# New step orders for every slot of a 58-slot interleaved kernel

## The chip, the core and the metric

The kernel runs on one core of a Trainium2 chip. A core has a matrix engine (PE in the profile, with PEld for its weight loads), a vector engine (DVE), an activation engine (ACT), a general engine (POOL), and SP, which here only issues DMAs. Each engine works through its own instruction list strictly in order and waits on semaphores. The metric is device time in microseconds (us), the median over executions.

## What is computed

The input x has 4 sequences of 512 tokens by 128 features. Twelve sub-blocks follow each other, each adding to x:

```python
x = x + 0.5 * L0_ffn(ln(x));  x = x + L0_attn(ln(x));  x = x + 0.5 * L0_ffn(ln(x))   # pattern FFN, local attention
x = x + 0.5 * L1_ffn(ln(x));  x = x + L1_attn(ln(x));  x = x + 0.5 * L1_ffn(ln(x))   # top-2 of 8 experts, linear attention
x = x + 0.5 * L2_ffn(ln(x));  x = x + L2_attn(ln(x));  x = x + 0.5 * L2_ffn(ln(x))   # routed experts, block attention
x = x + 0.5 * L3_ffn(ln(x));  x = x + L3_attn(ln(x));  x = x + 0.5 * L3_ffn(ln(x))   # two windowed layers, full attention
```

L3_ffn is two layers, so the kernel counts 14 sub-blocks.

## The kernel before

A *unit* is one sub-block on one sequence: 14 x 4 = 56 units, numbered 0 to 55, four sequences of a sub-block one after the other. A unit has three parts. *pre* normalizes x, projects it, makes bf16 pieces of q and k on DVE (`stack_parts`, L431 to L447) and turns them on PE (`turn_stacks`, L529). *core* is the attention or expert work. *post* projects the result back into x. The work is a software pipeline over *slots*: slot k holds the core of unit k (stream a), the pre of unit k + 1 (stream b) and the post of unit k - 1 (stream c). A few slots have further streams: in slots 0 to 2 DVE and SP prepare tables and fill a DRAM buffer (`make_tables`, `split_rows`, `fill_shear`, L2932 to L3012), and from slot 5 on POOL clears a set of semaphores (`keep`).

Each part is written as generators, one for each engine. A `yield` marks the start of a step, a step being some instructions with their semaphore waits. For each engine a merge puts the steps of the streams into one list, and so fixes the order in which that engine issues them. Within a stream the order is always the program's. Where a slot has a written order for an engine, `in_order` follows it: a string such as `c1a2b1` means one step of stream c, two of a, one of b. Where it has none, `weave` picks the stream whose next nominal time is smallest. Nothing else decides the order of work: the waits are in the steps and go with them.

```python
def merge(name, eng, streams, orders):
    if name in orders:
        in_order(name, eng, streams, orders[name])
    else:
        weave(name, eng, streams)
```

Slots -1 to 2 are each a block of their own that ends in a barrier of all engines. Slots 3 to 56 run in one block, where an engine that has finished its list of a slot goes on to the next; at the end of a slot it waits until POOL's `keep` of that slot has cleared a semaphore set (L3140 is the mark of an engine at a slot's end). Before the change slots 3 to 56 name an order (the entry of slot 56 is empty), and slots -1 to 2 are woven.

Lines that the prediction uses: L310 normalizes x with the result of POOL's L328; L336 turns it on PE and L343 (ACT) takes it; L387 to L401 project q, k, v; L606, L631 are PE work of post; L755, L978 spread a row over the partitions in the pattern FFN's post, L773 to L776 (DVE) and L784, L786 (PE) rank it, L820 and L837 (Gelu) are its pre; L1431 to L1437 (DVE), L1445 (ACT, Exp), L1392, L1406 (PE) are the core of the L0 attention; L1678, L1689, L1694 (PE), L1720 (DVE), L1701 (POOL) the core of the L1 attention.

Of the kernel before, what the change touches and what calls it, by code (L numbers as in the profile page):

```python
# [2383 lines left out]
def l3_layer_post(nc, m, lane, a, b, l):  # L2384
# [89 lines left out]
SLOT_ORDERS = {3: 0, 4: 1, 5: 2, 6: 3, 7: 4, 8: 5, 9: 6, 10: 7, 11: 8, 12: 9, 13: 10, 14: 11, 15: 12, 16: 13, 17: 14,  # L2474
# [3 lines left out]
ORDERS = [  # L2478
    {"tensor": "a5b1a1b1a1b1a1b1c1b1c1b1a1b1a1b2a1c1b1c1a1b2a1c1a3b1a3c1b1c1b1c1b1a1c1b1c1a1c1",
     "vector": "b4a2b5a3b1c2b1a1c1b1a1c1a1b1c4b1c2",  # L2480
     "scalar": "b3a1b2a1c1b3c1b8a1",
     "sync": "a1b5"},
    {"tensor": "b1a1b2c1a1b1a1c1b2a2b1a1b1a3b1c1a1b1c2a1b1c1b1a3b1a1c1b1a2b1c1b1c1b1c1a1c1a6",
     "vector": "b4a7b5a1c1a2b1a1c1a2b1c1a1c1a1b1a1c1a2b1a1c1a1c1a1c1a1c1a2b1c1",
     "scalar": "b3c1b2a1c1b2a1b2a2b1a2b1a3b1a2b4a9",
     "sync": "a4b5"},
    {"tensor": "b1a1b1c1b1c1b1a1b1a1c1b1a2b3a2b1c1a2b1a1b1c1a2b2a2b1a1b1a2b1c1a7",
     "vector": "b4c2a3b5a4b1c1a3b1a2b1c1a3b1a9b1c1",
     "scalar": "b7a1b2a1b1a2b1a2b1a3b1c1a1b1a1b1a2b1a7",
# [795 lines left out]
```

## Time and profile before

| what | value |
| --- | --- |
| median of 3 runs | 3191.61 us (3190.63 to 3198.51) |
| profiled execution | span 3199.9 us; no time is recorded for it besides the span |
| PE busy | 2706.5 us, 85% of the span |
| DVE busy | 2234.0 us, 70% |
| ACT busy | 1703.5 us, 53% |
| POOL busy | 846.5 us, 26% |
| mean granted TensorE clock | 0.896 of full speed |

Busy is the time in which an engine executes; where several waits end together the last one is named. PE is the busiest engine, and its idle time is the span less its busy time.

### The profile page before, as it was taken

Reading aid. Unit: us, or ns where it says so; the run is one execution under the profiler, and the core shown is the slowest. Engines: PE = TensorE matmul, PEld = TensorE weight load, DVE = VectorE, ACT = ScalarE, POOL = GpSimd, SP = SyncE. Lnnn points to the kernel's source line nnn. Section 1 sums busy time; section 2 is a strip of 40 time slices with the busy share of each in tenths; the row PEclk is TensorE's granted clock in tenths of the full one; section 3 lists DMA queues with packets and bytes.
Section 4 is the critical chain, followed back from the end, with each engine's and each line's share of the span. In section 5 each row is a group of like instructions: output and inputs, shape, how many; then the busy total and the mean of one; then the engine's idle time right before and its main releaser. Section 6 shows DMA issues by size and latency. Waiting matters only on the chain.

```text
span 3199.9 us, 64237 instructions
## 1 busy us (share of the span) xinstructions
PE 2706.5 (85%) x24501; PEld 1718.2 (54%) x24561; DVE 2234.0 (70%) x5316; ACT 1703.5 (53%) x4158; POOL 846.5 (26%) x875
## 2 busy tenths in 40 slices
PE   5857688898986789998877888899998988999996
PEld 2545455544443444457755787556563332465664
DVE  4756568778876677765566445798887777788883
ACT  2235443565622266643357434677765666676772
POOL 1010001122111221101232114565541112555550
PEclk8767787899977799998899989999998899999997
DMA  2523310000000000026710466110100000101010
GB/s 105 220 38 66 64 53 1 1 1 1 1 1 1 1 1 1 3 101 225 258 32 2 150 213 205 30 25 17 26 16 2 1 1 1 24 16 26 16 33 11
DMA packets 136844, 159.38 MB, mean 50 GB/s; under 512 B 84949, under 2 KB 111829, under 8 KB 135002
## 3 DMA queue, kind: packets, MB, share of 16 engines
q1 hardware_dynamic: 134010, 150.09, 15.7%
q8 instruction: 196, 3.21, 0.4%
q0 software_dynamic: 2048, 4.20, 0.4%
q10 hardware_dynamic: 480, 0.98, 0.1%
q14 instruction: 110, 0.90, 0.1%
HBM read 106.53 MB, written 30.61 MB: 43 GB/s over the span
## 4 chain that ended last, share of the span: by engine, by line
PE 48%; DVE 23%; ACT 9%; issue 7%; POOL 4%; DMA 3%; SPq 2%; DVEq 0%; POOLq 0%; ACTq 0%
DVE nm L1185 5%; PE ps L1144 3%; PE ps L529 3%; PE ps L1919 3%; PE ps L1121 3%; PE ps L2121 3%; ACT hand L494 3%; PE ps L1085 3%; PE ps L2287 3%; PE ps L387 2%; PE ps L606 2%; PE ps L266 2%; SPq L1368 2%; DVE pre L2207 2%; PE ps L1518 1%
## 5 line engine op out<-in xcount | busy, mean ns | idle before, releaser
L1185 DVE TENSOR_REDUCE nm<-ps 128x2 f32<-128x256 f32 (+2 forms) x704 | 427.6, 643 | 91.3 <-PE ps L1085 49.6
L1234 ACT ACTIVATE core<-ps 128x512 f32<-128x512 f32 x672 | 359.9, 589 | 92.6 <-PE ps L1126 56.7
L328 POOL TENSOR_TENSOR rstd<-ve,weights 128x4 f32<-128x4 f32 x80 | 81.0, 1013 | 869.7 <-DVE ve L305 865.7
L2193 POOL TENSOR_TENSOR pre<-pre,sin 128x512 f32<-128x512 f32 x128 | 238.1, 1879 | 255.4 <-ACT pre L2164 216.1
L1085 PE MATMUL ps<-hand 128*128 128x128 bf16 (+4 forms) x989 | 237.0, 315 | 42.6 <-DVE nm L1185 37.7
L494 ACT COPY hand<-ps 64x512 bf16<-64x512 bf16 x336 | 194.6, 579 | 136.9 <-PE ps L529 88.7
L1121 PE MATMUL ps<-hand 128*128 128x128 bf16 (+4 forms) x999 | 213.9, 303 | 11.2 <-ACT hand L494 6.3
L2327 ACT ACTIVATE core<-ps,nm 128x128 f32<-128x128 f32 x512 | 181.8, 376 | 67.8 <-DVE nm L2344 67.2
L2198 POOL TENSOR_TENSOR ss<-ss,weights 128x16 f32<-128x16 f32 x64 | 196.3, 3067 | 71.0 <-DVE ss L2213 69.1
L2121 PE MATMUL ps<-weights,pre 128*128 128x512 f32 x384 | 203.1, 631 | 5.7 <-ACT pre L2167 3.4
L1144 PE MATMUL ps<-core,hand 128*32 128x512 f32 (+3 forms) x2048 | 181.2, 449 | 8.1 <-ACT otok L1217 4.1
L1195 POOL CAST hand<-nm 128x16 bf16<-128x16 f32 x192 | 58.0, 302 | 461.7 <-DVE nm L1185 453.3
L1085 PEld LDWEIGHTS ps<-hand 128*128 128x128 bf16 (+1 forms) x1024 | 86.3, 99 | 160.9 <-DVE nm L1185 115.5
L529 PE MATMUL ps<-identb,hand 128*128 128x128 bf16 x768 | 84.7, 240 | 103.6 <-DVE pre L447 50.7
L1121 PEld LDWEIGHTS ps<-hand 128*128 128x128 bf16 (+1 forms) x1024 | 79.4, 97 | 161.0 <-ACT core L1234 88.2
L1919 PE MATMUL ps<-hand 128*128 128x128 f32 x1152 | 156.9, 296 | 1.9 <-DMA hand<-in_experts 1.6
L1919 PEld LDWEIGHTS ps<-hand 128*128 128x128 f32 x1152 | 150.8, 211 | 6.4 <-issue 3.1
L1935 ACT ACTIVATE core<-ps,hand 128x128 f32<-128x128 f32 x288 | 81.9, 369 | 126.6 <-PE ps L1919 117.1
L2287 PE MATMUL ps<-hand 64*64 64x128 f32 (+1 forms) x2048 | 134.7, 271 | 0.0
L1953 DVE SCALAR_TENSOR_TENSOR core<-ps,hand,core 128x128 f32<-128x128 f32 x288 | 80.8, 343 | 77.3 <-ACT core L1935 65.0
L529 PEld LDWEIGHTS ps<-identb,hand 128*128 128x128 bf16 x768 | 49.4, 105 | 151.9 <-DVE pre L447 57.6
L2424 PE MATMUL ps<-post,weights 128*128 128x512 f32 (+1 forms) x192 | 112.3, 668 | 18.3 <-DVE post L2451 10.4
(346 smaller groups left out, 6764.8 us busy)
## 6 DMA issues: line engine op xcount, KB each, us to landing
hand<-in_experts SPq DMA_DIRECT2D x72, 836.0 KB, 4.7
shear<-post SPq DMA_DIRECT2D x64, 256.0 KB
core<-in_experts SPq DMA_DIRECT2D x16, 836.0 KB, 7.8
core<-shear SPq DMA_DIRECT2D x256, 32.0 KB, 1.9
hand<-hand SPq DMA_DIRECT2D x16, 512.0 KB, 4.4
hand<-hand SPq DMA_DIRECT2D x16, 384.0 KB, 5.7
pre<-sorted_in SPq DMA_DIRECT2D x8, 704.0 KB, 4.9
sorted_out<-core SPq DMA_DIRECT2D x88, 64.0 KB
```

The costliest lines, as they stand in the source:

```text
L494: ins = copy(a.QX[64 * e:64 * e + 64, q_slot(2 * pair + e), :], src[64 * e:64 * e + 64, :])
L529: ins = nc.tensor.transpose(lane.atb[:, side * L + t * P:side * L + (t + 1) * P], pair_of(stk, t, pair), m.identb)
L1085: ins = nc.tensor.matmul(b[:, n * nk:(n + 1) * nk], q[:, qt * P:(qt + 1) * P], k[:, lo:lo + nk], start=kind != BLOCK32 and n == 0, stop=Tr ...
L1121: ins = nc.tensor.matmul(b[:, n * w:(n + 1) * w], k[:, kt * P:(kt + 1) * P], q[:, s:z], start=kind != BLOCK32 and n == 0, stop=True, skip_ ...
L1144: ins = nc.tensor.matmul(m.ps[32 * j:32 * j + 32, OUT, s:z], a.V[:, kt, 9 * h:9 * h + 32], prob8[:, i % PROBS, n * w:(n + 1) * w], start=( ...
L1185: nc.vector.tensor_reduce(nm_of(unit), src, AX.X, ALU.max, negate=True).then_inc(negmax, 1)
L1234: nc.scalar.activation(prob8[:, i % PROBS, 0:w], m.ps[:, RING[at % NR], 0:w], ACT.Exp).then_inc(ring_out, 1)
L1919: ins = nc.tensor.matmul(m.ps[:, 2 * (i % 2) + s, c * P:(c + 1) * P], w1(i, s, c), a.xs[:, i * P:(i + 1) * P], start=True, stop=True)
L2121: nc.tensor.matmul(banks[at % N], s.hT[:, t * P:(t + 1) * P], qkv[:, l, i, :], start=True, stop=True).then_inc(lane.filled, 1)
L2193: ins = nc.gpsimd.tensor_tensor(o[:, :, :, z:z + hl], x[:, :, :, y0:y0 + hl], sn[:, t, :, z:z + hl].unsqueeze(2).to_broadcast([P, 2, LH, h ...
L2198: nc.gpsimd.tensor_tensor(m.ss[:, 1, 0:2 * LH], m.ss[:, 0, 0:2 * LH], m.weight["half"][:, 0:2 * LH], ALU.pow).then_inc(rooted, 1)
L2287: ins = nc.tensor.matmul(out[rows, r * P + at:(r + 1) * P], a.Q3[rows, c, n * WIN:(n + 1) * WIN], a.K3[rows, c, lo:(n + 1) * WIN], start=F ...
```

## The change

Only the two tables `SLOT_ORDERS` and `ORDERS` change. Every slot from -1 to 56 now has an entry, and slots 3 to 55 that had orders get other ones for most engines. The steps, their instructions, their waits and the buffers are the same; only the interleaving of the streams on an engine differs. Slot -1 comes out as it was woven; slot 56 too. Over the slots, 1200 of 3037 PE steps, 1232 of 2808 DVE steps, 606 of 1996 ACT steps and 258 of 543 POOL steps stand at another place in their slot's list; most move by 1 to 5 places. The lists of slots 1 and 2 as they were woven are, for PE, `a1c1a2c1a1b1a1b1...` in both, for DVE `b3d2b1d2c3d1a1c1d1...` and `b4c3a1c1a1c1a2c1...`, and for ACT `c1b1c1b3a1b3a1b4a1` in both.

```diff
-SLOT_ORDERS = {3: 0, 4: 1, 5: 2, 6: 3, 7: 4, 8: 5, 9: 6, 10: 7, 11: 8, 12: 9, 13: 10, 14: 11, 15: 12, 16: 13, 17: 14,
+SLOT_ORDERS = {-1: 0, 0: 1, 1: 2, 2: 3, 3: 4, 4: 5, 5: 6, 6: 7, 7: 8, 8: 9, 9: 10, 10: 11, 11: 12, 12: 13, 13: 14,
...
 ORDERS = [
...
+    {"tensor": "a4b1a2b2a2b4a2b4a6b1a3b3a1b2a1b2",
+     "vector": "b4a4c1a2c2a1c1a1b1c1b8",
+     "scalar": "b3a1b6a1b2a1",
...
+    {"tensor": "a2b1c1a1d1c1a3c1a1c1a1b1c1b2c1b1a1b2c1b2c2b1a1b1c1a2c1a1b2a5b1a1b2a1b1a1b2",
+     "vector": "b3d2b1d6c4a3c2d1a1c1a1c1a1c1b1a1d2b1a1b6c1b1",
+     "scalar": "c2b1a1b10a2",
...
+    {"tensor": "c1a1c1b1a2b1c2a1b1a1c2a3c2b6a1c2a1b1a1b1a1c1a1b2a4b2a2b1a1b1a1b2",
+     "vector": "b4c7a2c1a4c1a1b2a1b6c1b1",
...
-    {"tensor": "b1a1b1c1b1c1b1a1b1a1c1b1a2b3a2b1c1a2b1a1b1c1a2b2a2b1a1b1a2b1c1a7",
-     "vector": "b4c2a3b5a4b1c1a3b1a2b1c1a3b1a9b1c1",
-     "scalar": "b7a1b2a1b1a2b1a2b1a3b1c1a1b1a1b1a2b1a7",
+    {"tensor": "c1a1b1a1c1b5c1a2b1a2b2a2b1a1c1b1a2b1a2b1a1c1b1a1b1a1b2a1c1a7",
+     "vector": "b4c1b4c1a1b1a6b1a3c1a2b1a3b1a2c1a1b1a1b1a5c1",
+     "scalar": "b8a1b1a1b1a2b1a5b1a1c1b1a1b3a9",
...
-     "scalar": "b7a3b1a1b3a5c1a11",
+     "scalar": "b5a1b2a2b1a1b3a5c1a11",
...
-    {"tensor": "c1a1c1b1a1b1a2b1a1b1a1b1a2c2b1a1b1a1b1a1b1a1b1a1b1a1b1a1b1a1b1a2",
-     "vector": "b4a8b19c1a1b1a2b1a2b1a2b1a2",
-     "gpsimd": "b1d1a1b6"},
+    {"tensor": "a2c1b2a3b2a1b1a2c3a1b1a1b1a1b1a1b2a1b1a1b1a1b1a1b1a2",
+     "vector": "b4a8b19a2c1b1a1b1a2b1a2b1a2",
+     "gpsimd": "d1a1b7"},
...
-    {"tensor": "a1c1a1c2a2c1b2a1b1a1b1a1b1a1b1a1b1a2b1a1b1a2b1a1b1a2b1a1b2",
+    {"tensor": "a4c2b1c1b1a1b1a1b2a1b1a2b1a2b1a1b1a2b1a1b1a1c1b1a1b1a1b1",
```

The orders shown are those of slots 0, 1, 2, 5, 7, 17 and 19, in this order.

## Rows read from the trace of the kernel before

**Rows 1.** Windows (from:to): length; PE, PEld, DVE, ACT, POOL busy; clock, DMA, GB/s.
```profile
209.00:429.00 220.00, 148.78 (x3905) 111.40 (x3906) 135.60 (x306) 101.89 (x206) 21.86 (x29) 0.74 0.39 62
580.00:880.00 300.00, 267.92 (x2189) 142.39 (x2217) 246.05 (x635) 184.46 (x378) 61.68 (x126) 0.98 0.01 1
880.00:1103.00 223.00, 167.79 (x1407) 95.52 (x1404) 146.32 (x331) 58.02 (x118) 37.28 (x46) 0.75 0.00 1
2005.00:2423.00 418.00, 385.74 (x3443) 250.97 (x3441) 343.33 (x623) 289.60 (x870) 210.16 (x107) 0.98 0.09 20
...
sum 3186.00, PE 2706.49 PEld 1718.17 DVE 2228.56 ACT 1703.46 POOL 838.76; mean PE 159.21 PEld 101.07 DVE 131.09 ACT 100.20 POOL 49.34
```

**Rows 2.** Waits of the whole span: us in total, times, longest.
```profile
PE ps L1085 <- DVE nm L1185: 37.7, 111, 1.3
```

**Rows 3.** Waits of PE in slots 4 to 7 (209 to 429 us).
```profile
PE ps L529 <- DVE pre L447: 16.6, 3, 8.6
```

**Rows 4.** Waits of PE in slots 16 to 19 (880 to 1103 us).
```profile
PE ps L529 <- DVE pre L447: 19.3, 3, 10.9
```

**Rows 5.** Timeline of slot 1, ACT, then DVE: start, us, what, [idle before].
```profile
91.19 0.58 ACT L343 COPY pre<-ps 128x512 f32<-128x512 f32 x1 [4.14 <-PE ps L336]
91.67 0.59 ACT L978 COPY post<-ps 128x512 f32<-128x512 f32 x1
...
92.38 0.29 DVE L773 TENSOR_SCALAR post<-post,acc 128x128 bf16<-128x128 f32 x1 [4.30 <-ACT post L978]
...
97.49 0.42 DVE L773 TENSOR_SCALAR post<-post,acc 128x384 bf16<-128x384 f32 x1 [2.91 <-PE ps L786]
...
100.78 0.68 DVE L3008 TENSOR_TENSOR cos<-pre 128x512 f32<-128x512 f32 x1
...
105.66 0.75 DVE L3012 TENSOR_TENSOR sin<-pre 128x256 f32<-128x256 f32 x2
```

**Rows 6.** Timeline of slot 5, DVE, ACT and PE.
```profile
272.86 1.17 DVE L310 TENSOR_SCALAR pre<-x,mv,rstd 128x128 f32<-128x128 f32 x4 [1.22 <-POOL rstd L328]
...
282.87 0.28 ACT L401 COPY hand<-ps 128x128 f32<-128x128 f32 x1
...
283.40 0.69 DVE L1431 TENSOR_TENSOR core<-ps,core 128x512 f32<-128x512 f32 x1 [2.64 <-DMA core<-shear]
...
285.46 0.42 DVE L431 CAST hand<-pre 128x512 bf16<-128x512 f32 x1
...
291.16 0.41 DVE L447 CAST pre<-pre 128x512 bf16<-128x512 f32 x1
...
291.63 0.61 PE L529 MATMUL ps<-identb,hand 128*128 128x128 bf16 x4 [6.34 <-DVE pre L447]
```

**Rows 7.** Timeline of slot 17, PE, DVE and POOL.
```profile
980.46 0.61 PE L529 MATMUL ps<-identb,hand 128*128 128x128 bf16 x4 [10.93 <-DVE pre L447]
...
981.42 0.40 PE L1678 MATMUL ps<-hand 64*128 64x128 bf16 x4
...
982.47 0.66 PE L1694 MATMUL ps<-core,hand 128*32 128x128 f32 x8
...
952.83 1.38 POOL L1701 MEMSET core<- 128x1536 f32 x1
952.91 3.72 DVE L310 TENSOR_SCALAR pre<-x,mv,rstd 128x128 f32<-128x128 f32 x4 [1.21 <-POOL rstd L328]
```

**Rows 8.** Timeline of slot 7, ACT: the table loads around Gelu (L837) and Exp (L1445).
```profile
398.37 1.28 ACT L1445 ACT_TABLE_LOAD   x1
399.66 1.15 ACT L1445 ACTIVATE core<-core 128x512 f32<-128x512 f32 x2
...
402.28 1.28 ACT L837 ACT_TABLE_LOAD   x1
403.57 0.60 ACT L837 ACTIVATE pre<-ps 128x512 f32<-128x512 f32 x1
```

**Rows 9.** Timeline of slot 41, PE.
```profile
2319.43 1.09 PE L2128 MATMUL ps<-weights,pre 128*128 128x128 f32 x8 [0.50 <-DVE pre L2226]
```

More of the change, by code:

```diff
@@ new lines @@
+    {"tensor": "b1c1b2a2b3c1b3a1b2a3b1a1b1a1c1b1c1b1a5c1a5b1a2b1a1c1b2",
+     "vector": "b4c2b4c1a6c1a1b2a1b3c1",
+     "scalar": "b11a2c1a1",
+     "gpsimd": "b1d1",
+     "sync": "a1"},
+    {"tensor": "c1a1c1a4b1a1c1b1a1c1a1b1c1b1c1b4a1b1a1c1b2c1b1a1c1a2c1b2a5b2a2b1a1b1c1b1",
+     "vector": "b3c1b1c3a1c1a3c1a2c1b2a1c1b1a1b1c1b5c1",
+     "scalar": "c2b3a1b8a2",
+     "gpsimd": "b1d1",
+     "sync": "a1"},
+    {"tensor": "a1c1a1c1a4c1a1c1b1a1b1c2b3c1b1a1b3a1c2b2c1a1c1b1a2b2a4b1a1b1a3b3",
+     "vector": "b4c5a4c3a1c1a1b2a1b1c1a1b6",
+     "scalar": "c2b2a1b9a2",
+     "gpsimd": "d1b1",
+     "sync": "a1"},
@@ new lines @@
+    {"tensor": "c3b1c1a1c2b1a3c1a1c1a1c1b1a1c1a2c1a1c1a2c1a1c1a2c1a1c1a5b1a1b2",
+     "vector": "b3c2b1c6a1b1c2a1c1b5c1b1c6a1c1a1c1b1a1c2b1a1c1b2a1c2a2c4a2c1a1c3",
+     "scalar": "b1c1a2b1c2a9b3",
+     "gpsimd": "b1d1c1b1c1",
+     "sync": "a9b1a3"},
+    {"tensor": "b1a2b1a4b1a13b2a2b1a1",
+     "vector": "b4a1b1a1b6a1b1a1b1c1b2a8",
+     "scalar": "b1a2b1a7b1a2b2",
+     "gpsimd": "b1e1c1b1",
+     "sync": "a7b1d1a5"},
+    {"tensor": "b2a6b1a16b3",
+     "vector": "b5a1b3a1b3c1a2b3a3b1a5",
+     "scalar": "b2a11b3",
+     "gpsimd": "b1c1b1d1",
+     "sync": "a9b1a3"},
@@ new lines @@
+    {"tensor": "a1b1a1b2a1b1a1b1a8b1a1b1a1b1a2b1a1b1a2b1a2b1a1b1",
+     "vector": "b4a1c1a2b3a1b5a1b3a2b1a1b1a2b1a2b1",
+     "scalar": "b1a1b1a1b2a1b1a2b3a2b1a1b1a1b1a2b1",
+     "gpsimd": "b2c1d1b5",
+     "sync": "a12"},
+    {"tensor": "a5b1a1b1a2b1a1b1a1b1a7b1a1b1a2b1a1b2a3b1a1b1a2b1a1",
+     "vector": "b1a1b2a3b1a5b3a1b1a1b4a2b2a1b1a1c1a1b4",
+     "scalar": "b5a3b1a2b2a2b1a3b1a1b1a4b1a3",
+     "gpsimd": "b2a2c1b3a1d1b2a1"},
+    {"tensor": "a4c1a2c1b2c1a1b1a2b1a1b1a7b1a3b2a1c1b1c1b1a3b1a1c1b1a2b1a1",
+     "vector": "b2a2b1a2c2b1a6b7a1b1a2b1a1b2a1c1a1b1c1b3c1",
+     "scalar": "b5a4b2a2b1a2b1a2b1a1c1b1a4b1a3",
+     "gpsimd": "b4a2b1d1a1b2a1"},
@@ new lines @@
+    {"tensor": "c1a5c1a1b2a1b1a2b1a1c1b1a1c1a6b1a2b1a1c1b1c1a1b2a3b1a1b1a2b1a1",
+     "vector": "b3a4c1b1a3c1a2c1a1b7a2b1a1b1a1b2a2c1b1c1b3",
+     "scalar": "b5a3b2a1b1a3b1a2c1a1b1a1b1a4b1a3",
+     "gpsimd": "b4a3b2d1b1a1"},
+    {"tensor": "a4b1c1a1b1c1a3b1a5c1a7c1a1c1a1b1a4b1a1c1b1a1",
+     "vector": "b3a2b1a2c1a1b2a1b5a1c1a3b4a4c1a2c2",
+     "scalar": "b2a11c1a4b1a1b1a1b1a1",
+     "gpsimd": "b1a2b1a1d1a1",
+     "sync": "b1"},
+    {"tensor": "c3b1c1b1a2b1a8c1a5c1a6b2a1b1",
+     "vector": "b2c1b1c1b1c1b7a3b2a1b1a1b1c1a4c1a3",
+     "scalar": "b2a6c1a5b3",
+     "gpsimd": "d1b2",
@@ L2633 @@
[L2633 to L2640 removed]
+    {"tensor": "b2a2b1a16b2a1b1a3",
+     "vector": "b11a4b3a1b1a1c1a6",
+     "scalar": "b2a9b2a2b1",
+     "gpsimd": "b1c1b1d1",
+     "sync": "a6b1a6"},
@@ L2693 @@
[L2693 to L2696 removed]
+    {"tensor": "c1a1c1a1b1c2a1b1a1b1a1b1a1b1c2a1c2a2b1c1b1a1b1c1b2c1a1b1c1b2",
+     "vector": "b4a2c1a3c5a1c1b7a1b2a1b2a1b1c2b1c1a1b1c1a1c1b1",
+     "scalar": "a2b1a1b1a1b1a1b2c1a1c1b2c1a1b1c1a2b1c1b1a1b2",
+     "gpsimd": "b1c1b1d1b4",
+     "sync": "c1"},
@@ L2722 @@
      "sync": "c1b1c1"},
     {"tensor": "a2b4a4b2a1b1a1b2a1b3a2",
-     "vector": "a2b2a2b4a1b1a3b3a1b2a2",
+     "vector": "a2b2a2b4a1b1a3b3a2b2a1",
      "scalar": "a5b1a1b1a1b1a1b2a2",
-     "gpsimd": "c1b1"},
-    {},
+     "gpsimd": "c1b1",
+     "sync": "b2"},
+    {"tensor": "a12",
+     "vector": "a12",
+     "scalar": "a5",
+     "gpsimd": "a1",
+     "sync": "a2"},
 ]
```

385 lines of the change are left out of this document (173 added, 212 removed), and 7 rows, old and new, of the table SLOT_ORDERS.

## The prediction

> **What bounds the kernel now.** I read the windows by stage first, then the waits of PE, then timelines of single slots beside the strings of the diff. The windows [rows 1] say two things. PE is the busiest engine in every stage listed, and how far it is from being the bound differs: it idles 32.1 of 300 us in slots 12 to 15 (580 to 880) and 32.3 of 418 us in the L3 layers of slots 36 to 43, but 71.2 of 220 us in slots 4 to 7 (L0 attention) and 55.2 of 223 us in slots 16 to 19 (L1 attention), where its granted clock is also lower, 0.74 and 0.75 against 0.98. Over all windows it idles 3186.0 - 2706.5 = 479.5 us. An order can give back only idle time, so that is the pot, and a good part of it is where no order helps, such as the first load and the last slot.
>
> The waits say what kind of idle time it is. In the attention slots of L1 and L2 type it is many short waits: 111 waits on DVE's maxima come to 37.7 us, 0.34 us each [rows 2]. In slots 4 to 7 and 16 to 19 it is a few long ones: PE's turns of q and k (L529) wait 16.6 us and 19.3 us for the last step of the DVE chain of pre (L447), three times each, up to 10.9 us [rows 3, 4]. A long wait can be used in two ways: the chain that it waits for can be served earlier, or other steps can be put into it.
>
> **The change part by part.** Instructions, waits and transfers stay, so no duration is added or removed; what changes is which waits are filled and which are made. I take the slots in four groups.
>
> *Slots 0 to 2*, woven before. In slot 1 the ACT list had the L343 of pre ahead of post's second L978; it sat until 91.19 and L978 ended at 92.26, which is what DVE's ranking waited for, 4.30 us long [rows 5]. The new ACT list begins `c2b1`, the new DVE list does six of the table steps (L2994 to L3012) right after its normalization (`b3d2b1d6`), and the new PE list takes post's ranking counts earlier (`c1` at place 10 instead of 14). First, L978 no longer stands behind L343: at least the 0.58 us of L343, at most the 4.30 us; I take 1.5, because PE still has two matmul steps of the core before the second L755. Second, 0.68 + 0.75 us of tables go into the 4.30 us wait: 1.4. Third, of the 2.91 us in which DVE waits for L786 I take a third, 1.0: 3.9 us in slot 1 [rows 5]. Slot 2 has the same lists without tables: 2.5. Slot 0 I leave at 0, between +2.9 (a new wait as long as the one seen) and -2.9. Sum -6.4, bounds +3 and -14.4 (4.30 + 2.91 in both slots). SP's list of slot 2 has its waits after other issues of the fill, and nothing in the slot waits for these; that costs nothing unless the slot's barrier comes to wait for SP, and then no more than a DVE wait here, 2.91, inside the +3.
>
> *Slots 4 to 7.* In slot 5 the projection ends on ACT at 282.87 + 0.28 = 283.15, but DVE has three steps of the core ahead of the chain, the first of which waits 2.64 us for its DMA, so the chain runs from 285.46 to 291.57, 6.1 us [rows 6]. The new DVE list has all but the last step of the chain before the core's first (`c1b4c1a1b1`), with one step of post and one of the core (0.69) inside it. Then it can end near 283.15 + 6.1 + 2 x 0.69 = 290.6, 0.9 us earlier, and the PE list also moves two steps of post out from between the projections, for which I take 1.1 us more. That is 2 us in slot 5 and, as an estimate by likeness, in 4 and 6: -6. What is late next is the core's first three DVE steps, by up to the 6 us of the chain; PE then has the turns of pre to do, which is the cover, and if it is gone the gain goes back to 0. Slot 7 goes the other way. Its new ACT list puts one Exp of the core between Gelus (`b5a1b2a2` for `b7a3`). Each change of function brings a table load of 1.28 us [rows 8], so two more loads, 2.6 us in all; ACT waits 1.2 us or so for PE between these Gelus in the before profile, so I charge 1.4. Sum -4.6, bounds -16.6 (the whole wait of rows 3) and +4.
>
> A rule speaks against that step. The Trainium skill, ScalarE: Activation LUTs, section What ACT_TABLE_LOAD costs, says that a switch costs a load and then a drain, some 2.66 us together; by that the two loads would be 5.3 us and the sum of this part 2.7 us worse. The trace does not agree: the load starts at 398.37, takes 1.28, and the Exp starts at 399.66; the Gelu starts at 403.57 after a load from 402.28 [rows 8].
>
> *Slots 16 to 19.* In slot 17 PE stands idle for 10.93 us before the first turns at 980.46 and then does a step of the core (L1678, L1689, L1694) from 981.42 to 983.13, 1.7 us, which needs only what DVE had finished before its chain [rows 7]. The new PE list has that step ahead of the turns (`c3a1b1`), so it goes into the wait: -1.7. POOL's list has its 1.38 us memset ahead of L328 instead of behind it; there it runs beside the four L310, which take 3.72 us against 1.17 us in slot 5 [rows 6, 7]. Three smaller memsets still follow, so of the 2.55 us I take 1.0. That is -2.7 in slot 17, the same in 18, -1.1 in 19 (one step of post leaves the stretch before the turns) and 0 in 16: -6.5. Bounds: -19.3, the whole wait of rows 4, and +3 for one new wait like DVE's 2.91 [rows 5].
>
> *All others.* Two steps in five have another place, but mostly by 1 to 3, and where PE is nearly full there is little to fill: late in slot 41 the one wait seen is 0.50 us [rows 9]. The idle time outside the two attention stages is 479.5 - 71.2 - 55.2 = 353.1 us. I take -5, near nothing, because the short waits of rows 2 are those of two engines in lockstep, which an order does not undo; bounds -30 (a tenth, rounded down) and +15 (44 more waits of 0.34 us).
>
> The sum is -6.4 - 4.6 - 6.5 - 5 = -22.5 us. Against the profiled execution's span of 3199.9 that is 3177.4. The median of the runs shown is 8.3 us below that span; taking the difference as the same after, I predict 3191.6 - 22.5 = 3169 us, 0.7% faster. The bounds add up to -80.3 and +25, 3111 and 3217.
>
> **The rivals.** *Nothing to measure.* The slot may be as long as its chain from pre's normalization to its last turn, and steps put into a wait were then off the path anyway. For it: the long waits all end with the same DVE chain, whose own 6 us no order shortens. Against: in slot 5 the chain starts 2.3 us after its input is there. By this only the serving of chains counts, about 0.9 us in slots 4 to 6, and what slots 0 to 2 give is eaten by slot 7: 3191.6 - 2.7 = 3189 us. Chance 0.20.
>
> *Slower.* An engine in order stops for a step that is put ahead of its producer, and all that is behind it stops too. 1200 PE steps are moved. If one in ten of them, 120, waits a lockstep wait of 0.34 us more [rows 2], PE loses 41 us, less the 22.5 gained: 3191.6 + 18.5 = 3210 us. It decides from 66 such steps, one in eighteen. For it: much of the time is in slots where PE is 90% busy, which can lose more than win. Against: in the slots that I followed, the steps moved ahead had their inputs. Chance 0.16.
>
> *Much faster.* The granted clock in the two idle-rich stages is 0.74 and 0.75, and elsewhere up to 0.98 [rows 1]. If fewer long pauses of PE let it be granted 0.10 more there, its busy time falls by 148.8 x (1 - 0.74/0.84) = 17.7 and 167.8 x (1 - 0.75/0.85) = 19.7 us, and if PE was the bound there, the time by 37 more: 3132 us. Against: only three long waits in each stage, and they shrink without going away. Chance 0.10.
>
> **How the numbers follow.** The forecast, from 10 to 45 us faster, has 0.54; its own range is 3147 to 3182. Within 0.3% (9.6 us, about what a measurement of this kernel can tell from no change) has 0.20. Faster is 0.54 + 0.10 = 0.64, slower 0.16. For eight times in ten the range takes the forecast, the case of no change, the nearer half of the fast one and part of the slow one: 3130 to 3204.
>
> **What the next profile would show.** If the steps are right: PE's wait for L447 in 209 to 429 falls from 16.6 to about 12 and in 880 to 1103 from 19.3 to about 14; slots 1 and 2 are 2 to 4 us shorter each; in slot 17 L310 takes less than 3.72; ACT has two table loads more, in slot 7; the stages with a clock of 0.98 stay within 1% of their length. The prediction is wrong if waits of PE on DVE L1185 or on ACT grow by more than 20 us in the attention stages, if the pre chain is served earlier but the core's turns (L1392) wait as much longer, or if the clock moves.

## The result, and the profile after

The changed kernel takes 3226.32 us in the median (3224.43 to 3232.85, 4 runs) against 3191.12 us before: the ratio is 1.0117, 95% interval 1.0102 to 1.0131. It is 1.2% slower where 0.7% faster was forecast.

The page of its profiled execution begins so:

```profile
span 3223.3 us, 64234 instructions
## 1 busy us (share of the span) xinstructions
PE 2709.1 (84%) x24501; PEld 1714.5 (53%) x24561; DVE 2252.0 (70%) x5316; ACT 1706.1 (53%) x4160; POOL 838.5 (26%) x875
```

PE is about as busy as before (2706.5 us), so nearly all of the longer span (20.8 of 23.4 us) is idle time of PE; DVE is busy 18 us longer for the same instructions. Between these two executions the difference is 3223.3 - 3199.9 = 23.4 us. Between the medians it is 35.2, because the profiled execution of before lay 8.8 us above its median and that of after 3.0 below.

The windows of the stages after, cut where PE passes from one slot to the next as in [rows 1]: slots 4 to 7, slot 8 alone, 12 to 15, 16 to 19, 36 to 43.

```profile
198.34:414.59 216.25, 149.07 (x3928) 111.70 (x3930) 136.50 (x307) 104.16 (x208) 21.23 (x29) 0.74 0.38 63
414.59:456.14 41.55, 32.64 (x209) 20.34 (x199) 15.76 (x54) 13.26 (x27) 0.00 (x0) 0.79 0.20 77
573.38:879.32 305.94, 267.31 (x2183) 142.42 (x2214) 251.96 (x643) 184.69 (x378) 61.42 (x127) 0.99 0.01 1
879.32:1100.25 220.93, 171.37 (x1413) 98.46 (x1406) 142.77 (x322) 57.37 (x118) 37.00 (x46) 0.75 0.00 1
2010.89:2433.75 422.86, 387.71 (x3430) 252.18 (x3430) 345.87 (x622) 289.31 (x870) 204.96 (x107) 0.98 0.09 20
```

Slot 4 begins at 198.34 instead of 209, and the attention stage behind it is 4 us shorter: at the end of slot 7 the changed kernel is 14.6 us ahead. Then it loses 38.0 us. Slot 8 takes 41.55 us (34.5 before), slots 12 to 15 are 5.9 us longer, slots 36 to 43 5.4 us. Worked out from the marks of PE in the same way, stage by stage, after less before. (The written tables are longer now, so what stood behind them stands 38 lines lower in the changed kernel: the mark L3140 is L3178 there.)

| slots | length | of it idle time of PE |
| --- | --- | --- |
| -1 to 3 | -10.6 | -4.0 |
| 4 to 7 | -4.0 | -4.0 |
| 8 to 11 | +8.5 | +6.7 |
| 12 to 15 | +5.9 | +6.5 |
| 16 to 19 | -2.0 | -5.6 |
| 20 to 23 | +8.7 | +7.0 |
| 24 to 27 | -0.7 | -1.2 |
| 28 to 31 | +8.6 | +5.4 |
| 32 to 35 | -8.0 | -1.9 |
| 36 to 43 | +5.4 | +2.9 |
| 44 to 47 | +7.2 | +3.6 |
| 48 to 55 | +4.6 | +5.3 |

The waits that the prediction named, after: of the whole span, then of slots 4 to 7 and of 16 to 19.

```profile
PE ps L1085 <- DVE nm L1185: 46.0, 126, 2.0
...
PE ps L529 <- DVE pre L447: 15.1, 3, 7.7
...
PE ps L529 <- DVE pre L447: 13.8, 2, 8.7
```

Against [rows 2 to 4] PE waits 8.3 us more for DVE's maxima, and 1.5 and 5.5 us less for the chain of pre.

**Slot 1** went as forecast. ACT and DVE there, after:

```profile
88.53 0.59 ACT L978 COPY post<-ps 128x512 f32<-128x512 f32 x1 [1.40 <-PE ps L755]
89.01 0.59 ACT L343 COPY pre<-ps 128x512 f32<-128x512 f32 x1
...
88.11 0.68 DVE L3046 TENSOR_TENSOR cos<-pre 128x512 f32<-128x512 f32 x1
88.71 0.75 DVE L3050 TENSOR_TENSOR sin<-pre 128x256 f32<-128x256 f32 x2
89.38 0.28 DVE L773 TENSOR_SCALAR post<-post,acc 128x128 bf16<-128x128 f32 x1
```

L978 now runs ahead of L343, the tables (L3046 and L3050, which were L3008 and L3012 before) stand where DVE waited 4.30 us [rows 5], and L773 begins without a wait. The 2.91 us wait behind it is gone too. From its first instruction to its last, slot 1 takes 33.7 us instead of 39.1, slot 2 32.8 instead of 36.2, slot 0 39.3 instead of 41.1.

### The profile page after: what moved, and what is told of

Read it like the earlier page. It is cut to its first block, busy times and chain, and to the rows that moved or that the text cites. A ratio compares the mean times of both kernels' runs of the same rounds, so it can differ in the third digit from the quotient of the medians.

```text
span 3223.3 us, 64234 instructions
## 1 busy us (share of the span) xinstructions
PE 2709.1 (84%) x24501; PEld 1714.5 (53%) x24561; DVE 2252.0 (70%) x5316; ACT 1706.1 (53%) x4160; POOL 838.5 (26%) x875
## 4 chain that ended last, share of the span: by engine, by line
PE 45%; DVE 27%; ACT 9%; issue 8%; POOL 3%; DMA 2%; SPq 1%; DVEq 0%; POOLq 0%; ACTq 0%
DVE nm L1185 5%; PE ps L1144 3%; PE ps L529 3%; PE ps L1085 3%; PE ps L1121 3%; PE ps L1919 2%; DVE pre L2207 2%; PE ps L387 2%; PE ps L606 2%; ACT hand L494 2%; PE ps L2430 2%; PE ps L2121 2%; PE ps L266 2%; PE ps L2287 2%; PE ps L1518 2%
## 5 line engine op out<-in xcount | busy, mean ns | idle before, releaser
L1185 DVE TENSOR_REDUCE nm<-ps 128x2 f32<-128x256 f32 (+2 forms) x704 | 428.6, 649 | 102.6 <-PE ps L1085 58.4
L328 POOL TENSOR_TENSOR rstd<-ve,weights 128x4 f32<-128x4 f32 x80 | 82.6, 1032 | 914.7 <-DVE ve L305 877.5
L2193 POOL TENSOR_TENSOR pre<-pre,sin 128x512 f32<-128x512 f32 x128 | 232.3, 1834 | 241.7 <-ACT pre L2164 218.1
L1085 PE MATMUL ps<-hand 128*128 128x128 bf16 (+4 forms) x986 | 239.8, 318 | 49.7 <-DVE nm L1185 46.0
L1121 PE MATMUL ps<-hand 128*128 128x128 bf16 (+4 forms) x1002 | 218.1, 307 | 16.4 <-ACT hand L494 8.8
L2198 POOL TENSOR_TENSOR ss<-ss,weights 128x16 f32<-128x16 f32 x64 | 194.3, 3036 | 68.8 <-DVE ss L2213 66.9
L1085 PEld LDWEIGHTS ps<-hand 128*128 128x128 bf16 (+1 forms) x1024 | 88.0, 100 | 168.4 <-DVE nm L1185 122.6
L1121 PEld LDWEIGHTS ps<-hand 128*128 128x128 bf16 (+1 forms) x1024 | 80.8, 98 | 161.4 <-ACT core L1234 83.0
L529 PEld LDWEIGHTS ps<-identb,hand 128*128 128x128 bf16 x768 | 49.6, 104 | 146.7 <-DVE pre L447 52.9
```

The source lines that it names most:

```text
L529: ins = nc.tensor.transpose(lane.atb[:, side * L + t * P:side * L + (t + 1) * P], pair_of(stk, t, pair), m.identb)
L1085: ins = nc.tensor.matmul(b[:, n * nk:(n + 1) * nk], q[:, qt * P:(qt + 1) * P], k[:, lo:lo + nk], start=kind != BLOCK32 and n == 0, stop=Tr ...
L1121: ins = nc.tensor.matmul(b[:, n * w:(n + 1) * w], k[:, kt * P:(kt + 1) * P], q[:, s:z], start=kind != BLOCK32 and n == 0, stop=True, skip_ ...
L1185: nc.vector.tensor_reduce(nm_of(unit), src, AX.X, ALU.max, negate=True).then_inc(negmax, 1)
L2193: ins = nc.gpsimd.tensor_tensor(o[:, :, :, z:z + hl], x[:, :, :, y0:y0 + hl], sn[:, t, :, z:z + hl].unsqueeze(2).to_broadcast([P, 2, LH, h ...
L2198: nc.gpsimd.tensor_tensor(m.ss[:, 1, 0:2 * LH], m.ss[:, 0, 0:2 * LH], m.weight["half"][:, 0:2 * LH], ALU.pow).then_inc(rooted, 1)
```

## The experiments

All kernels below differ from the kernel before only in the two order tables; the last three also cut one memset. A ratio is to the kernel before, from runs on the same chip. The runs are from several chips, on which the median of the kernel before lay between 3189 and 3198 us, so two rows are compared by their ratios.

| run | us | ratio, 95% interval |
| --- | --- | --- |
| changed kernel | 3226.3 | 1.0117 (1.0102 to 1.0131) |
| first | 3176.4 | 0.9947 (0.9933 to 0.9962) |
| rest | 3256.6 | 1.0194 (1.0177 to 1.0210) |
| attend8 | 3226.4 | 1.0114 (1.0090 to 1.0138) |
| slot8 | 3221.1 | 1.0096 (1.0079 to 1.0112) |
| fixes | 3219.3 | 1.0065 (1.0042 to 1.0088) |
| peold | 3299.9 | 1.0321 (1.0299 to 1.0343) |
| dveold | 3293.4 | 1.0302 (1.0278 to 1.0325) |
| actold | 3265.5 | 1.0217 (1.0180 to 1.0254) |
| poolold | 3221.9 | 1.0092 (1.0064 to 1.0119) |
| best | 3143.9 | 0.9850 (0.9819 to 0.9880) |
| losers | 3264.6 | 1.0212 (1.0178 to 1.0245) |
| split_after | 3213.8 | 1.0075 (1.0054 to 1.0096) |
| split_before | 3191.7 | 0.9999 (0.9982 to 1.0016) |
| split_best | 3143.5 | 0.9867 (0.9846 to 0.9887) |

### Where the loss sits

```diff
 first:   new orders for slots -1 to 7, old ones for 8 to 56
 rest:    old orders for slots -1 to 7, new ones for 8 to 56
 attend8: new orders for slots 12 to 15, 20 to 23, 28 to 31, 44 to 47 only
```

> New orders in slots -1 to 7 alone, the old ones in 8 to 56. Sum of slots (each slot's list costs or gives what it does, wherever it runs): the profile of the changed kernel stood 14.6 us ahead at the end of slot 7, so 15 us less than before, about 3176 us, ratio 0.995. Rival, the budget of the clock: the time gained early is paid back in the later slots although their orders are the old ones, so within 4 us of before.

> Old orders in slots -1 to 7 (the first four woven), the new ones in 8 to 56. Sum of slots: the loss of slots 8 to 56 without the early gain, 38 us between the two profiles and up to 50 us between the medians (35.2 + 14.6), so 3229 to 3241 us, ratio 1.012 to 1.016. Rival, the budget of the clock: the late slots lost because the early ones were fast, so here the loss is well under 30 us.

> New orders only in slots 12 to 15, 20 to 23, 28 to 31 and 44 to 47 (the lockstep attention of eight heads), the old ones elsewhere. Sum of slots: these sixteen slots grew by 5.9 + 8.6 + 8.6 + 7.2 = 30.3 us between the two profiles, so about 3221 us, ratio 1.0095. Rival, the loss of these slots is the scatter of one profile or comes from their neighbours: within 10 us of before.

The three runs gave 0.53% less, 1.94% more and 1.14% more. The first is 17 us by its ratio, for a sum of slots of 15. The early gain stays when the rest is old, so the idea that the clock pays it back falls. The loss belongs to slots 8 to 56, and more than half of it to the sixteen slots of the eight-head attention (36 us by the ratio, for a sum of 30). The second run lost 62 us by its ratio, more than its sum of 38 to 50; the section on the hardware takes that up.

The profiles show how firmly a length belongs to a slot and its order. Lengths of eight slots in us, six that repeat well and two (16 and 39) that do not, worked out from PE's marks in seven profiles; the letter says whose order the slot has there (o old, n new):

| slot | before | first | attend8 | after | rest | best | losers |
| --- | --- | --- | --- | --- | --- | --- | --- |
| 8 | 34.5 o | 34.4 o | 34.4 o | 41.5 n | 40.8 n | 34.6 o | 41.8 n |
| 13 | 74.3 o | 74.3 o | 81.0 n | 80.4 n | 81.4 n | 74.3 o | 79.8 n |
| 18 | 50.8 o | 50.9 o | 50.8 o | 42.0 n | 41.9 n | 42.0 n | 48.2 o |
| 29 | 45.0 o | 45.0 o | 49.5 n | 49.7 n | 49.7 n | 45.0 o | 49.5 n |
| 40 | 52.2 o | 52.2 o | 52.2 o | 50.6 n | 50.6 n | 50.4 n | 52.5 o |
| 54 | 51.5 o | 51.5 o | 51.5 o | 55.6 n | 55.6 n | 51.5 o | 55.4 n |
| 16 | 67.8 o | 63.1 o | 62.7 o | 71.5 n | 71.5 n | 63.8 o | 71.4 n |
| 39 | 52.0 o | 52.0 o | 52.0 o | 58.0 n | 55.0 n | 52.0 o | 57.6 n |

The six rows are not the rule. Of the 96 pairs of a slot from 8 to 55 and one of its two sets of lists, 31 agree within 0.3 us in these seven profiles, but 51 differ by more than 1 us from profile to profile and 23 by more than 2 us, the most slot 34 with old lists (46.2 to 54.7). A difference of 1 or 2 us between two profiles of one such slot says little about its lists.

Taking for every slot the median length with either order (in the profiles of before, after, first, rest, attend8 and slot8, but for slot 8 of the last), 12 of the slots 8 to 56 get shorter by 29 us together and the others longer by 81: +52. Slots -1 to 7 give -15.6. That is +36, against 35.2 between the medians. Of the 52 us in slots 8 to 56, 31 are idle time of PE and the other 21 are PE's own busy time, for the same matmuls; where this was looked at below, the granted clock was lower there.

### A choice by slot

```diff
 best:   new orders for slots -1 to 6, 10, 14, 18, 20, 25, 32, 36, 40, 41, 51, 52
 losers: new orders for all the others
```

> A choice by slot: the new lists in slots -1 to 6, 10, 14, 18, 20, 25, 32, 36, 40, 41, 51 and 52, whose lengths were shorter with them in the profiles so far, the old ones in all others. Sum of slots: the differences of these slots add up to -45 us, so 3191 - 45 = 3146 us, ratio 0.986. Rival, lists that fit only their new neighbours and a clock that takes back in one slot what is saved in the other: less than half of it, above 3168 us.

> The opposite choice: old lists in slots -1 to 6, 10, 14, 18, 20, 25, 32, 36, 40, 41, 51 and 52, the new ones in all others. Sum of slots: the differences of these add up to +82 us, so about 3273 us, ratio 1.025. Rival as in the run of the opposite choice: far from that sum, under 3240 us.

The choice came out at 3143.9 us, 1.5% faster than before: 48 us by the ratio (38 to 58 by its interval), for a sum of slots of 45. The opposite choice is 2.1% slower: 68 us (57 to 78), short of its sum of 82 us. Both are far on the other side of what the rival foretold (above 3168, under 3240), so lists put between neighbours of the other kind keep, taken together, most of what they cost or give; the rival falls. For a single slot that need not hold. Slot 14 with its new lists (79.8 us) was chosen over the old ones at 81.4 and 81.7 us, where the clock was 0.96; in the run losers the old lists had the clock 1.00 and took 78.5 us. This choice is the version that beats both kernels.

### Slot 8: one step before its transfer

```diff
-    {"tensor": "b1c1b2a2b3c1b3a1b2a3...
+    {"tensor": "b1c1b5c1b3a3b2a3...
```

> The changed kernel, but in slot 8 PE does the core's first two steps after nine steps of pre instead of after three, so that the 5.03 us wait for the transfer of in_stream lies beside six projections. If that wait was the whole cost of slot 8: 5 to 7 us less than the changed kernel, about 3220 us, ratio to before 1.009 to 1.010. Rival, a chain of slot 8 that the wait only uncovers: 0 to 2 us less.

PE in slot 8: before, after, and in this run (the idle time is in brackets); ahead of them the issue of the transfer in the changed kernel.

```profile
415.60 0.36 SPq L870 DMA_DIRECT2D core<-in_stream  x1
...
423.25 3.75 PE L879 MATMUL ps<-core,wv 128*128 128x512 f32 x4 [5.03 <-DMA core<-in_stream]
```

```profile
439.32 1.95 PE L879 MATMUL ps<-core,wv 128*128 128x512 f32 x4 [0.20 <-DMA core<-in_stream]
```

```profile
424.13 2.81 PE L879 MATMUL ps<-core,wv 128*128 128x512 f32 x6 [0.38 <-DMA core<-in_stream]
```

The transfer is issued about 1 us into the slot and PE can go on with its data 7.65 us later. The old list asked for it after nine steps of pre (the turn L336 and eight steps of L820), the new one after three; in the kernel before and in the run slot8 it landed 9.0 and 9.1 us after its issue, 0.2 and 0.4 us after PE had got there. In the new order the matmuls behind the wait are slow as well (3.75 us for four L879 against 1.95; the granted clock is 0.50 there and 1.00 in the two other kernels), so a 5.03 us wait costs 7 us. With two steps moved, slot 8 takes 34.4 us (41.5; before 34.5): the whole cost of slot 8 is this one place. The kernel came to 1.0096 for 1.0117; that is the 5 to 7 us expected, but the two intervals overlap, and it is the slot's length that shows it.

### Six slots mended by hand

```diff
 slot 8   "tensor": as above
-slot 13  "vector": "b2a3c1b1a3...    "gpsimd": "b2a1c1b2a1...
+slot 13  "vector": "b3a3c1a3...      "gpsimd": "b3a1b1c1a1...
-slot 29  "vector": "b2a2b1a2c2b1...
+slot 29  "vector": "b2a4b1c2b1...
-slot 30  "vector": "b3a4c1b1a3...
+slot 30  "vector": "b2a4b1c1b1a3...
-slot 54  "tensor": ...b1c1a2b2c1b1c1b2
+slot 54  "tensor": ...b1c1b2c1a2b1c1b2
-slot 16  "tensor": "c1a1c1b1c1a1c2b1...
+slot 16  "tensor": "c1a1c1a1c2b1c1b1...
```

> The changed kernel with six slots mended, each read by its own length (from the last mark of PE to the next), against the lengths of the changed kernel. Slot 8 as in the run slot8 (41 to 34.5 us). Slot 13 (80.4): DVE's third step of pre (L305) before POOL's 3.51 us memset begins instead of inside it, and POOL's next memsets behind the rstd of post. Slots 29 and 30 (49.6, 46.7): L305 two to four steps later, so that DVE does its maxima during the memset. Slot 54 (55.6): the core's steps 10 and 11 (which wait 2.75 us for DVE) behind post's step 11. Slot 16 (71.5): the steps that were done ahead of pre's turn of x (L336) before are ahead of it again. If single misplaced steps are the cause: 13 falls by 3 to 6, 29 and 30 by 1 to 4 each, 54 by 2 to 4, 16 by 4 to 8 (most of it clock), 8 by 6.5; together 20 us or more under the changed kernel, near 3200 us. Rival, many small waits in lockstep: only slot 8 falls, 13, 29 and 30 by under 1, and the kernel stays above 3215 us.

Two of the six came out: slot 8, and slot 13 from 80.4 to 76.1 us (74.3 with the old lists). Slots 29 and 30 (49.6 and 46.6) and 16 (71.4) did not move, slot 54 grew from 55.6 to 57.1 and slot 55 behind it from 43.4 to 46.7. The kernel came to 3219.3 us, above the 3215 that was to speak for many small waits.

*Slot 13.* DVE and POOL in the changed kernel, near the start of the slot and at post's normalization:

```profile
646.22 1.92 DVE L305 TENSOR_SCALAR ve<-mv 128x4 f32<-128x4 f32 x1
646.29 1.85 DVE L1185 TENSOR_REDUCE nm<-ps 128x1 f32<-128x384 f32 x2
...
644.61 3.51 POOL L510 MEMSET hand<- 128x4096 f32 x1 [15.52 <-ACT otok L1217]
...
665.12 2.40 DVE L310 TENSOR_SCALAR y<-y,mv,rstd 128x128 f32<-128x128 f32 x4 [0.16 <-POOL rstd L328]
...
665.26 0.95 POOL L460 MEMSET hand<- 128x1024 bf16 x1
```

before, and in the mended kernel:

```profile
651.17 2.13 DVE L1185 TENSOR_REDUCE nm<-ps 128x1 f32<-128x384 f32 x4
...
649.55 3.51 POOL L510 MEMSET hand<- 128x4096 f32 x1 [15.72 <-ACT otok L1217]
```

```profile
635.01 0.17 DVE L305 TENSOR_SCALAR ve<-mv 128x4 f32<-128x4 f32 x1
...
637.21 1.78 DVE L1185 TENSOR_REDUCE nm<-ps 128x1 f32<-128x384 f32 x3
```

L305 is a 128x4 instruction of 0.17 us. Issued while POOL clears 4096 columns it ends only when that ends, at 648.1, and the maxima queued behind it on DVE end there too. The maxima themselves are not slowed by it: before, four of them ran in 2.13 us, most of it while the same memset ran. PE's waits for the maxima (L1085 for L1185) come to 4.4 us in this slot for 1.4. The Trainium skill (SBUF — State Buffer, section SBUF: two separate sides) calls the port pair that DVE and POOL share an exclusive lock, held for a whole instruction; the trace agrees, 648.14 for the end of L305 against 648.12 for that of the memset. L310 takes 2.40 us beside POOL's next memsets, 1.18 before. PE's turn (L336) then waits 2.2 us for L322 where it had waited 0.2.

*Slot 54* shows why hand mending failed. The waits of PE in it, after and mended:

```profile
PE ps L2298 <- DVE core L2352: 2.8, 1, 2.8
```

```profile
PE ps L2424 <- DVE post L2451: 3.9, 1, 3.9
```

Moving PE's step behind the wait only let PE arrive at the next product of DVE too early. Both waits are for DVE. DVE and POOL after, and DVE's L310 before:

```profile
3100.13 3.02 DVE L310 TENSOR_SCALAR post<-post,mv,rstd 128x128 f32<-128x128 f32 x4 [0.90 <-POOL rstd L328]
...
3120.29 0.17 DVE L2221 TENSOR_SCALAR ss<-ss 128x16 f32<-128x16 f32 x1 [2.01 <-POOL ss L2198]
...
3122.13 1.54 DVE L2352 TENSOR_TENSOR core<-core,rsum 128x512 f32<-128x512 f32 x1
...
3100.07 2.48 POOL L2193 TENSOR_TENSOR pre<-pre,sin 128x512 f32<-128x512 f32 x2
```

```profile
3085.34 1.11 DVE L310 TENSOR_SCALAR post<-post,mv,rstd 128x128 f32<-128x128 f32 x4
```

POOL's new list has post's L328 ahead of two L2193 (`b3c1b3` for `b5c1b3`), so L310 starts beside L2193 and takes 3.02 us instead of 1.11, and DVE's list then puts a step that waits 2.01 us for POOL's L2198 ahead of the L2352 and the second L2451 that PE wants. With POOL's old list alone this slot is 53.2 us (next group): 2.4 of its 4.1 us. In slot 16 too one wait took another's place: the 1.3 us for pre's L310 became 2.7 us for post's L642 (0.5 in the changed kernel), and DVE's list had not been changed.

### One engine's lists at a time

```diff
 peold:   changed kernel, old PE lists in 8 to 56 but 9, 23, 29, 32, 36, 37, 44, 45, 46, 54
 dveold:  changed kernel, old DVE lists in 8 to 56 but 10, 16, 19, 24, 44, 45, 54
 actold:  changed kernel, old ACT lists in 8 to 56 but 23, 25, 32, 44, 45, 49, 54
 poolold: changed kernel, old POOL lists in 8 to 56
```

> The changed kernel with PE's old lists in 38 of the slots 8 to 56 (all but 9, 23, 29, 32, 36, 37, 44, 45, 46, 54, 55, where PE's list stays new), the other engines' lists new. Those slots have 37.6 us of the loss. If PE's steps stand ahead of their producers and that alone costs: 30 us or more come back, 3190 to 3200 us. If it is DVE's or POOL's lists: under 10 us come back, 3217 us or more.

> The changed kernel with DVE's old lists in slots 8 to 56 but 10, 16, 19, 24, 44, 45 and 54, the other engines' lists new. Those slots have 30.1 us of the loss. If DVE's lists cost (steps that fall into POOL's memsets, producers served later): 20 us or more come back, about 3205 us. If PE's lists cost alone: PE still asks in the new order and DVE no longer serves it, so the same or slower than the changed kernel, 3226 us or more.

> The changed kernel with ACT's old lists in slots 8 to 56 but 23, 25, 32, 44, 45, 49 and 54, the other engines' lists new. If the four engines' lists of a slot only work as a set, as PE's and DVE's do: slower than the changed kernel by 20 us or more, 3246 us or more. If ACT, busy 53% of the time, has room enough for either order: within 10 us of the changed kernel.

> The changed kernel with POOL's old lists in slots 8 to 56, the other engines' lists new. If the places of POOL's memsets and of L2193 beside DVE's steps are what stretches DVE (134.5 us of stretch in the profile after, 103.6 before): 10 us or more come back, 3216 us or less, and the stretch goes back to about 105. Rival: POOL's lists cost nothing, within 5 us of the changed kernel.

I had wanted to learn which engine's list costs. The answer is that the question is wrong for PE, DVE and ACT. Going back to the old list on one of them, where old is the better order in most slots, does not bring time back; by the ratios it costs 65, 59 and 32 us more than the change itself. PE's waits for DVE's maxima, 37.7 us before and 46.0 in the changed kernel, are 46.3 us with DVE's lists taken back and, the longest, with PE's:

```profile
PE ps L1085 <- DVE nm L1185: 54.3, 135, 2.1
```

Slot 13, for instance, is 74.3 us with four old lists, 80.4 with four new ones, and 84.7, 80.6 and 81.7 with PE's, DVE's or ACT's old list among new ones. The lists of a slot belong together, so these runs cannot share the loss out among the engines. With POOL's lists back, the mean ratio is 0.25% lower than that of the changed kernel, and the two intervals overlap: a gain of up to some 18 us, or none. Slot 13 (78.3), 54 (53.2) and 21 (81.3) get shorter by it, slots 40 (55.9 for 50.6) and 18 (47.9 for 42.0) longer. DVE's hold-up, worked out as in the next group, is 126 us there for 134.5 in the changed kernel, not the 105 that I expected.

### How much is DVE held up by POOL

For every DVE instruction I take its time less the time of the same instruction when it runs fast (the tenth part from below), where that is over 0.1 us. Instructions queued behind each other are each counted, so a stretch can be in the sum more than once; DVE's busy time grew by 18 us. The sum is 103.6 us before and 134.5 after; of it 17.0 and 28.1 lie beside POOL's L510 alone, 44.4 and 53.5 beside L2193. The last three runs cut L510 in four:

```diff
-        nc.gpsimd.memset(a.whole[:, 0:4096], 0.0).then_inc(cleared, 1)
+        for s in range(0, 4096, 1024):
+            ins = nc.gpsimd.memset(a.whole[:, s:s + 1024], 0.0)
+        ins.then_inc(cleared, 1)
```

> The changed kernel, with POOL's memset of 4096 columns (L510, 3.51 us) cut into four of 1024; all lists as they are. If DVE's hold-up beside this memset makes a good part of the loss: the stretch beside it falls from 28.1 to under 12 us, slots 13, 29 and 30 (80.4, 49.7, 46.7) get 1 to 4 us shorter each, and the kernel 8 us or more faster than the changed one, 3218 us or less. Rival: DVE's hold-ups lie beside waits that would be there anyway; the stretch falls but the kernel stays within 4 us of the changed one.

> The kernel before with the same memset in four pieces. The stretch beside it was 17.0 us, so by the hold-up theory 2 to 5 us less than before; by the rival no change within 4 us.

> The mixed choice of lists by slot (3144 us) with the memset in four pieces. Its slots 13, 29 and 30 have the old lists, so as in the kernel before: 2 to 5 us less by the hold-up theory, no change by the rival. Ratio to before 0.983 to 0.985.

The stretch beside the memset fell to 3.6 us in the changed kernel and 1.9 in the kernel before. Yet slots 13, 29 and 30, where I looked for it, stayed at 80.8, 49.8 and 46.7 us. The four L310 behind it, beside the next memsets (L460 to L462), now took 2.77, 2.78 and 2.78 us in them, for 2.40, 1.76 and 1.47 with the whole memset, so a part of the hold-up moved on. Slot 29, in the changed kernel and with the memset cut:

```profile
1678.59 1.76 DVE L310 TENSOR_SCALAR pre<-x,mv,rstd 128x128 f32<-128x128 f32 x4
```

```profile
1675.25 2.78 DVE L310 TENSOR_SCALAR pre<-x,mv,rstd 128x128 f32<-128x128 f32 x4 [0.30 <-POOL rstd L328]
```

The kernel came to 1.0075, 0.4% under the changed kernel. By the slots of its profile the gain is in slot 21 (83.3 to 79.3) and in slots 16 to 19 (220.9 to 214.0, of which 4.3 are PE's busy time; 6.9 of it in slot 19, which took 49.8 us in the run losers with the same lists and the whole memset), and slot 14 lost 5.5 us again, at a lower clock. The kernel before and the best one did not change beyond their intervals. So cutting this memset takes some 5 to 21 us off the changed kernel, by the two intervals, and in other slots than I had named; part of that is the clock. The hold-up beside L2193 was not tried alone.

## Why the prediction was wrong

**Slots 0 to 2** (-6.4): right, and larger. Slot 1 gave 5.4 us (3.9 forecast), slot 2 3.4 (2.5), slot 0 1.8 (0). The waits of slot 1 that the working named are filled or gone, as it said.

**Slots 4 to 7** (-4.6): -4.0. The sum came out by luck; its parts, 2 us in each of slots 4 to 6, did not: slot 4 gave 3.4, slot 5 1.3, slot 6 0.1. In slot 5 the chain does follow its input at once, as the working said. But the projection, which was to end 1.1 us earlier by PE's list, ends 11.9 us into the slot instead of 10.6. So the chain starts at 12.0 us instead of 12.9, takes 6.9 us instead of 6.1 and ends at 18.9 instead of 19.0: no gain. PE's wait for L447 in the four slots went from 16.6 to 15.1 us only, not to 12. Slot 7 has six table loads instead of four and is 0.8 us longer (1.4 forecast).

**Slots 16 to 19** (-6.5): -2.0, and for other reasons. In slot 17 L310 does take less, 2.41 us for 3.72 [rows 7], and the wait for L447 falls from 10.9 to 8.7; but PE's list puts the turn of x (L336) where it waits 2.7 us longer for DVE, and the slot grows by 2.9. Slot 16 grows by 3.7. Slot 18 alone gives 8.9, of which 2.7 are busy time of PE, which the working did not count.

**All others** (-5, between -30 and +15): +40.1 between the two profiles. This is the step that failed. It held that steps which move by 1 to 3 places where PE is nearly full win or lose little, and it priced a loss as 44 more lockstep waits of 0.34 us. The runs showed three things in its place. First, one place can hold a long wait: slot 8, 7 us, for a transfer that I had not followed; the run slot8 shows it. Second, the shift of waits is broad, which the profiles show and no run takes apart: in slots 8 to 56 PE has 598 waits of over 0.06 us for 581, and those under 1 us came to 205.4 us for 180.5. Slots 13 and 54 show a kind of it: one engine's list asks for a product before another engine's list, POOL's hold-up included, can deliver it. Third, I priced waits by their length; in slots 8 to 56 PE's busy time grew too, by 9.2 us between the two profiles and 21 by the medians of the slots.

**The rivals.** "Nothing to measure" (3189 us, chance 0.20) is out: the change is clear of the noise. "Slower" at 3210 us had chance 0.16 and the right sign, and its mechanism, PE ahead of its producers in order, is that of slots 8 and 54; how much of the rest it makes is not shown. It came out 16 us short: it set a loss of 41 us against a gain of 22.5, where the medians of the slots give 52 against 15.5, and it left the clock out. "Much faster" needed another clock in the attention stages: it stayed 0.74 and 0.75. Of what was to show the prediction wrong, the first sign, 20 us more of waits on L1185 or on ACT, did not come (8.3 on L1185 over the whole span, 5 on ACT in the attention stages). Of what was to show it right, this failed: the stages with a clock of 0.98 did not stay within 1%, 12 to 15 grew by 2.0% and 36 to 43 by 1.3%.

What stays open: how much of the new idle time in slots 8 to 56 (31 us by the medians of the slots) comes from the lists alone and how much from DVE held up beside POOL's L2193, and what decides where the clock falls in slot 16, which kept 71.4 us when its first wait was moved.

## What to carry to other kernels

The lists of the engines for one stage are one schedule: change them together, compare stage by stage from marks at the stage ends, and keep the better set for each stage. Here that turned a loss of 1.2% into a gain of 1.5%, for 1.4% by the sum of the stages. Take more than one profile of each set, and look at the clock of a stage before its length is believed. When an order is forecast, follow every stage's first consumer of a transfer, and count a gain in three stages as nothing against forty stages that were not looked at.

## What the runs showed of the hardware

**A wait of PE costs more than its length where the clock falls behind it.** Slot 18 in windows of some 10 us, before and after; the third column from the right is the granted clock (0.5 is 1.2 GHz, 1.0 is 2.4):

```profile
997.60:1007.60 10.00, 5.87 (x37) 3.31 (x37) 6.73 (x19) 1.24 (x3) 4.62 (x7) 0.80 0.01 2
1007.60:1017.60 10.00, 10.00 (x73) 4.31 (x72) 2.99 (x5) 1.89 (x9) 0.00 (x0) 0.52 0.00 0
1017.60:1027.60 10.00, 7.14 (x77) 4.98 (x73) 8.15 (x18) 1.69 (x4) 0.00 (x0) 1.00 0.01 2
1027.60:1037.60 10.00, 4.04 (x38) 2.58 (x38) 8.20 (x14) 3.15 (x5) 3.28 (x3) 0.50 0.00 1
```

```profile
1003.97:1013.97 10.00, 7.14 (x64) 4.19 (x64) 6.92 (x21) 2.53 (x9) 4.76 (x7) 1.00 0.01 2
1013.97:1023.97 10.00, 7.98 (x82) 4.41 (x74) 6.43 (x15) 2.32 (x7) 0.00 (x0) 0.93 0.00 0
1023.97:1033.97 10.00, 7.98 (x65) 5.37 (x63) 9.43 (x18) 2.29 (x5) 2.76 (x3) 0.56 0.01 2
```

Before, PE is busy 5.87 us of the first 10 and works the next 10 at 0.52; a 5.8 us wait follows and again 0.50. PE's longest waits in it:

```profile
PE ps L1694 <- ACT otok L1731: 5.8, 1, 5.8
PE ps L529 <- DVE pre L447: 3.1, 1, 3.1
PE ps L336 <- DVE pre L310: 2.6, 2, 1.9
```

After, the longest wait is 2.0 us and the first 20 us run at 1.00 and 0.93. The slot is 8.9 us shorter, of which 6.1 are idle time and the rest is PE's busy time (36.1 to 33.4). Slot 39 goes the other way: PE has a 1.9 us wait for L2451 near the end of slot 38, the clock falls behind it, and slot 39 takes 58.0 us with 3.4 of idle time. In the run rest the same lists have the same 1.9 us wait, but the clock stays at 1.00 across the boundary, and slot 39 takes 55.0 us with the same 3.4. So this wait does not by itself decide whether the clock falls. The stretches on both sides of the boundary, in the changed kernel and in the run rest:

```profile
2156.84:2166.84 10.00, 7.75 (x49) 5.49 (x48) 7.84 (x9) 2.19 (x4) 6.70 (x3) 0.79 0.40 92
2166.84:2176.84 10.00, 10.00 (x75) 8.53 (x75) 2.32 (x5) 4.83 (x13) 0.00 (x0) 0.70 0.01 2
```

```profile
2190.85:2195.85 5.00, 3.61 (x25) 3.05 (x26) 4.12 (x7) 0.14 (x1) 2.98 (x2) 1.00 0.42 105
2195.85:2200.85 5.00, 5.00 (x51) 4.37 (x50) 1.73 (x4) 2.89 (x6) 0.00 (x0) 1.00 0.02 3
```

**The clock also falls at other places from one run to the next.** Slot 14 with the same lists and the same DVE and ACT work, in the run rest and in the changed kernel:

```profile
742.02:827.41 85.39, 76.90 (x556) 38.20 (x551) 67.87 (x182) 45.88 (x96) 17.77 (x33) 0.92 0.00 1
```

```profile
723.71:803.55 79.84, 69.93 (x549) 36.28 (x551) 67.78 (x182) 45.80 (x96) 17.74 (x33) 1.00 0.00 1
```

That is 5.5 us in one slot. It goes far to explain why the run rest was slower than the sum of its slots: its slots 12 to 15 took 313.9 us against 305.9, with 12.7 us more of PE's busy time, and its slots 8 to 56 took 18.9 us more than in the changed kernel, with 26.7 us more of PE's busy time. So the same lists in these slots can differ, from one profile to another, by more than half of the 35 us that the change cost.
